# A two-layer attention kernel on one core: weight products behind their own loads, band values in pairs, first loads and statistics moved ahead of three stage borders

## The reference, cut to what matters

```python
x = L0_attn_x                                   # (2, 2048, 256)
xn = _layernorm(x, axis=-1)
s = _L0_attn_ref(xn, ...)                       # 16 heads of 16, full softmax over 2048 tokens
g = _silu(_L0_ffn_ref(xn, ...))                 # 8 experts, low rank, cumulative sum over tokens, forward + inverse branch
x = x + s * g
xn = _layernorm(x, axis=-1)
s = _L1_attn_ref(xn, ...)                       # the same heads, |q - k| <= 64
g = _silu(_L1_ffn_ref(xn, ...))                 # gated LoRA with 8 experts
x = x + s * g
```

## Time and profile before

| | us |
|---|---|
| median of 3 runs | 2538.43 (2525.03 to 2546.25) |
| the profiled execution, device time | 2525.01 |
| its span in the profile | 2523.4 |
| mean granted TensorE clock | 0.942 of full |
| PE busy | 2223.5 (88%) |
| DVE busy | 1840.8 (73%) |
| ACT busy | 1448.0 (57%) |
| POOL busy | 462.9 (18%) |

### The profile page before, as it was taken

One profiled execution on the slowest core, in us unless ns is written; L12 is line 12 of the kernel. 1 busy time (PEld: TensorE's weight loads), 2 busy tenths in 40 slices (PEclk: granted clock), 3 DMA queues, 4 the chain that ended last, 5 costly groups with the idle time before them and its releaser, 6 DMA issues. The chain is left out here.

```text
span 2523.4 us, 44312 instructions
## 1 busy us (share of the span) xinstructions
PE 2223.5 (88%) x14912; PEld 1229.1 (49%) x14912; DVE 1840.8 (73%) x3240; ACT 1448.0 (57%) x2165; POOL 462.9 (18%) x673
## 2 busy tenths in 40 slices
PE   4588689999999999999999999988999966799988
PEld 3456333333333333333333333327888855555578
DVE  1655589999999999999999999913443465798736
ACT  2344257777777777777777777771222222266643
POOL 0000000000000000000000000003554510266645
PEclk9799679999999999999999999998999988698889
DMA  3567820040230400500404102006666269876365
GB/s 121 198 237 260 137 26 3 12 55 3 34 33 5 62 5 8 60 3 21 47 5 51 16 5 62 3 5 189 159 164 180 67 239 333 150 148 139 82 183 161
DMA packets 189122, 231.81 MB, mean 92 GB/s; under 512 B 72721, under 2 KB 122769, under 8 KB 186065
## 3 DMA queue, kind: packets, MB, share of 16 engines
q1 hardware_dynamic: 176048, 210.46, 34.2%
q10 hardware_dynamic: 7184, 14.10, 3.0%
q0 software_dynamic: 5728, 5.00, 0.9%
HBM read 138.97 MB, written 89.13 MB: 90 GB/s over the span
## 5 line engine op out<-in xcount | busy, mean ns | idle before, releaser
L967 DVE TENSOR_REDUCE a_maxes<-a_ps_a 128x2 f32<-128x1024 f32 x1024 | 1202.2, 1221 | 112.8 <-PE a_ps_a L1088 109.0
L1032 ACT ACTIVATE a_prob<-a_ps_s 128x512 f32<-128x512 f32 (+1 forms) x1376 | 1036.2, 805 | 348.4 <-PE a_ps_s L1114 342.4
L1114 PE MATMUL a_ps_s<-a_Q,a_K 50*128 50x512 f32 x2048 | 593.4, 453 | 89.8 <-ACT a_prob L1032 89.7
L1088 PE MATMUL a_ps_a<-a_K,a_Q 48*128 48x512 f32 x2048 | 551.2, 455 | 25.2 <-DMA a_Q<-s_halves 14.1
L1126 PE MATMUL a_ps_o<-a_prob,a_V 128*17 128x512 f32 x4096 | 541.5, 601 | 0.1
L1114 PEld LDWEIGHTS a_ps_s<-a_Q,a_K 50*128 50x128 f32 x2048 | 277.2, 185 | 504.9 <-ACT a_prob L1032 456.9
L1088 PEld LDWEIGHTS a_ps_a<-a_K,a_Q 48*128 48x128 f32 x2048 | 245.1, 189 | 230.7 <-issue 107.9
L925 POOL DMA_DIRECT2D a_Q<-a_m_parts x128 | 64.3, 502 | 1282.3 <-DVE a_m_parts L959 1278.6
L1532 ACT ACTIVATE a_prob<-a_ps_s 128x512 f32<-128x512 f32 (+1 forms) x256 | 136.2, 583 | 128.0 <-PE a_ps_s L1623 124.6
L1473 DVE CUSTOM_DVE_ANT_0 a_scratch<-a_ps_a,k_mask 128x256 f32<-128x256 f32 (+1 forms) x512 | 176.7, 410 | 41.6 <-PE a_ps_a L1587 41.6
L1587 PE MATMUL a_ps_a<-a_K,a_Q 48*128 48x256 f32 (+1 forms) x512 | 124.1, 369 | 32.5 <-DMA a_Q<-s_halves 31.6
(11 more groups left out here) (184 smaller groups left out, 2212.2 us busy)
## 6 DMA issues: line engine op xcount, KB each, us to landing
s_halves<-p_parts SPq DMA_DIRECT2D x64, 512.0 KB, 5.2
s_xT<-p_xT SPq DMA_DIRECT2D x64, 256.0 KB, 4.4
a_K<-s_halves SPq DMA_DIRECT2D x63, 256.0 KB, 7.0
c_xT<-s_xT SPq DMA_DIRECT2D x48, 256.0 KB, 5.3
a_Q<-s_halves SPq DMA_DIRECT2D x186, 64.0 KB, 10.3
s_v<-p_v_out SPq DMA_DIRECT2D x16, 544.0 KB, 4.5
s_cT<-p_cT SPq DMA_DIRECT2D x32, 256.0 KB, 3.6
k_wb<-s_w SPq DMA_DIRECT2D x16, 512.0 KB, 7.7
```

Source lines behind the costliest of these rows:

```text
L967: nc.vector.tensor_reduce(maxes[:, :, slot, qt, kc], ps_a[:, o:o + 2 * CH].rearrange("p (z k) -> p z k", z=2), AX.X, ALU.max).then_inc(a_d ...
L1032: nc.scalar.activation(prob[:, ring:ring + len(t), :].rearrange("p r q -> p (r q)"), ps_s[:, bank:bank + len(t) * CH], ACT.Exp, scale=scal ...
L1088: last = nc.tensor.matmul(ps_a[:, o + side * CH:o + (side + 1) * CH], Q[rows, q0:q0 + P], K[rows, k0:k0 + CH], start=True, stop=True)
L1114: last = nc.tensor.matmul(ps_s[:, bank + x * CH:bank + (x + 1) * CH], K[rows, k0:k0 + P], Q[rows, q0:q0 + CH], start=True, stop=True)
```

## The change

Six edits:

- In `phase_weights` the loads are sorted into eleven groups with a semaphore each, the three arrays of the inverse first. PE waits for a group only before the product that needs it; the router products come before the expert products. The seven plain splits are done behind products 4, 8, 11 and 13. The bias rows have their own semaphore.
- The buffers and semaphores of a projection's first rows move out of `phase_project` into `row_buffers` (the rows lie in the weight buffer `wb`, which is idle then). The first two chunks of x are loaded, measured and rooted, and the first is normalised, inside `phase_weights`.
- The same is done for layer 1 in the last chunk of `phase_combine_experts`.
- The first 24 loads of K and Q for the band are issued near the end of `phase_project(layer 1)`, 12 (`first_halves`) and 12 (`second_halves`), half by SP and half by ACT.
- In the band, values are multiplied for two steps at a time, at even steps; ACT's copies go with them, PE's turns and DVE's normalisation follow at odd steps. RING, the number of buffers for exponentials, goes from 5 to 6.
- In the last two groups of the band SP loads the first four chunks of transposed tokens and two chunks of rows for `phase_combine_lora`.

```diff
+        loads = {
+            "inverse": [(square["WinvT"][:], "W_invT"), (square["WQ"][:], "W_Q"), (square["WK"][:], "W_K")],
+            "router": [(square["W1T"][:], "router_w1T")],
+            "Vf": [(wide["Vf"][:], "V_fwd")], "Vi": [(wide["Vi"][:], "W_inv_exp")],
+            "qkv0": [(raw_qkv[:, 0], "w_qkvT_0")],
...
+        PLAIN_AT = {4: (0,), 8: (1,), 11: (2,), 13: (3, 4, 5, 6)}
...
+            for g, group in loads.items():
+                for dst, key in group:
+                    sp.dma_start(dst, I[key].rearrange("(k p) n -> p k n", p=P)).then_inc(loaded[g], DMA)
+                if g in ("router", "Vi"):
+                    load_rows(sp, L, I["x"], 0, 0 if g == "router" else 1)
...
-            pe.wait_ge(loaded, DMA * n_loads)
+            have("inverse")
...
+            row_statistics(nc, dve, L, 0, 0, passed)
             for j in range(N_SPLIT):
...
+                for i in PLAIN_AT.get(j, ()):
+                    plain_low_part(i)
+                if j == 1:
+                    row_statistics(nc, dve, L, 0, 1, passed)
+                if j == 2:
+                    normalise_rows(nc, dve, L, 0, 0)
...
+        def first_halves(eng, side):
+            if KQ:
+                for m in range(4):
+                    wait_apart(eng, parts_stored[m], DMA * 2 * (NCH - 1), passed)
+                load_first(eng, S, KQ, side)
...
+                    if not more and u == 0:
+                        first_halves(sp, 0)
                     store_parts(sp, i, u)
                     if after:
                         store_turned(sp, *after)
+                    if not more and u == 1:
+                        second_halves(sp, 0)
                     store_values(sp, i, u)
...
+                    if not more:
+                        (second_halves if u else first_halves)(act, 1)
...
-    RING = 5
+    RING = 6
...
             def prefetch(g, k):
+                wait_apart(sp, s_ready, 2 * (KT * g + 2 * k + 2), passed)
                 if g + 2 < NG:
-                    wait_apart(sp, s_ready, 2 * (KT * g + 2 * k + 2), passed)
-                    load_next(sp, 0, g + 2, k)
+                    load_next(sp, S, KQ, 0, g + 2, k)
+                elif k < 4:
+                    for x in range(2):
+                        load_lora_turned(sp, S, KQ, (g + 2 - NG) * 2 + k // 2, k % 2, x)
+                elif g + 2 == NG:
+                    load_lora_rows(sp, KQ, KQ["x"], x_dram, k - 4)
...
-                if 0 <= s - LAG < STEPS:
-                    add_values(s - LAG)
-                if 0 <= s - LAG - 1 < STEPS:
-                    for cc in ends_at(s - LAG - 1):
-                        turn_output(cc)
+                if s % 2 == 0 and LAG < s < STEPS + LAG:
+                    for earlier in (s - LAG - 1, s - LAG):
+                        add_values(earlier)
+                if s % 2 == 1 and LAG + 1 < s:
+                    for earlier in (s - LAG - 2, s - LAG - 1):
+                        for cc in ends_at(earlier):
+                            turn_output(cc)
...
+                else:
+                    wait_apart(sp, mul1, FT * c + HALF_FT, passed)
+                    for u in range(2):
+                        load_rows(sp, L, out_dram, 0, u)
...
+                if c == CHUNKS - 1:
+                    for u in range(2):
+                        row_statistics(nc, dve, L, 0, u, passed)
                 for t in range(TT):
                     n = TT * c + t
+                    if c == CHUNKS - 1 and t == 1:
+                        normalise_rows(nc, dve, L, 0, 0)
```

More of the change, by code:

```diff
@@ L181, in _, with have @@
             last.then_inc(high, 1)
[L183 to L185 removed]
         @block.tensor
         def _(pe):
[L189 removed]
+            def have(g):
+                pe.wait_ge(loaded[g], DMA * len(loads[g]))
+            have("inverse")
             for m, src in ((0, WQ), (1, WK)):
@@ L197, in _ @@
             pe.wait_ge(high, 2)
+            have("router")
             j = 0
+            for t in range(DK):
+                for r, left in enumerate((WQ, WIQ)):
+                    for k in range(DK):
+                        o = (2 + j % 6) * CH + r * D
+                        last = nc.tensor.matmul(bank[:, o:o + D], left[:, k, t * P:(t + 1) * P],
+                                                square["W1T"][:, k, :], start=(k == 0),
+                                                stop=(k == DK - 1), skip_group_check=True)
+                last.then_inc(product, 1)
+                j += 1
             for left, right in ((WQ, "Vf"), (WIQ, "Vi"), (WK, "Wf"), (WIK, "Wi")):
+                have(right)
                 for t in range(DK):
@@ L208, in _ @@
                     j += 1
-            for t in range(DK):
-                pe.wait_ge(low, j - 5)
-                for r, left in enumerate((WQ, WIQ)):
-                    for k in range(DK):
-                        o = (2 + j % 6) * CH + r * D
-                        last = nc.tensor.matmul(bank[:, o:o + D], left[:, k, t * P:(t + 1) * P],
-                                                square["W1T"][:, k, :], start=(k == 0),
-                                                stop=(k == DK - 1), skip_group_check=True)
-                last.then_inc(product, 1)
-                j += 1
+            have("out")
             for half in range(4):
@@ new lines, in row_statistics @@
+def row_statistics(nc, dve, L, i, u, passed):
+    c = 2 * i + u
+    dve.wait_ge(L["x_loaded"][u], DMA * (i + 1))
+    for t in range(TT):
+        nc.vector.bn_stats(L["stats"][:, u, t], L["xn"][:, u, t]).then_inc(L["stat"], 1)
+    wait_apart(dve, L["stat"], (TT + 1) * c + TT, passed)
+    for t in range(TT):
+        last = nc.vector.bn_aggr(L["mean_var"][:, u, t], L["stats"][:, u, t])
+    last.then_inc(L["stat"], 1)
+    dve.wait_ge(L["stat"], (TT + 1) * (c + 1))
+    nc.vector.tensor_scalar(L["var_eps"][:, u], L["mean_var"][:, u, :, 1], EPS, None, ALU.add
+                            ).then_inc(L["eps_ready"], 1)
@@ L334, in phase_project @@
         ps_l = n.ps("ps_l", CH) if first else None
[L339 to L343 removed]
+        xn_ready = L["xn_ready"]
         t_ready = n.sem("t_ready")
@@ new lines, in load_first, with load_second, load_next @@
+def load_first(eng, S, KQ, side):
+    for k in range(PAIR + 1):
+        load_keys(eng, S, KQ, side, 0, 0, EARLY_K, k, KQ["early"])
+    for k in range(PAIR + 1):
+        load_queries(eng, S, KQ, side, 0, 0, k, KQ["early"])
+def load_second(eng, S, KQ, side):
+    for k in range(PAIR + 1):
+        load_keys(eng, S, KQ, side, 0, EARLY_K, T, k, KQ["loaded"][0])
+    for k in range(PAIR + 1):
+        load_queries(eng, S, KQ, side, 0, 1, k, KQ["loaded"][0])
+def load_next(eng, S, KQ, side, g, k):
+    done = KQ["loaded"][g % BAND_BUFS]
+    if k % 2 == 0:
+        load_keys(eng, S, KQ, side, g, 0, T, k // 2, done)
+    else:
+        load_queries(eng, S, KQ, side, g, 0, k // 2, done)
+        load_queries(eng, S, KQ, side, g, 1, k // 2, done)
@@ L2011, in _ @@
                         bias(c, ft // 2 - 1)
+                if c == CHUNKS - 1:
+                    for u in range(2):
+                        inverse_root(pool, W, L, u, u)
                 for t in range(TT):
```

370 lines of the change are left out of this document (178 added, 192 removed).

## The result

| | before | after |
|---|---|---|
| median, us | 2538.4 (2525.0 to 2546.3, 4 runs) | 2471.4 (2462.9 to 2482.3, 4 runs) |
| ratio, with its 95% interval | | 0.976 (0.972 to 0.980) |
| profiled execution: device time, span | 2525.0, 2523.4 | 2464.9, 2463.2 |
| mean granted TensorE clock in it | 0.942 | 0.952 |

The change makes the kernel faster, and by more than was forecast: 2471 lies 7 us under the low end of the range, 2478. Run again twice, the changed kernel stood at 0.9759 and 0.9763 of the kernel before, so some 60 us are the change's own; the 67 us of the first medians are those and a little luck. By the sum's own measure, span against span, 37 us were forecast and 60.2 came.

What follows compares the result with a forecast made beforehand. Loads bound the first 27.4 us; in the band DVE is the limit at 2.4 GHz, PE at 1.2. Sum: −33.2 − 9.2 + 0.8 + 11 − 6.4 = −37.0, from 2525.0 to 2488 us; range 2478 to 2522.

Steps and rivals of the forecast that it cites:

- Weights and first projection: Start of kernel: PE starts after three arrays, fewer splits remain, rows are already normalised; −33.2 us (−27 to −36).
- rival 3: Weights stage: PE runs the weight products at 1.2 GHz, stopping between load groups; −23 us, 2515; chance 0.05.
- Experts to second projection: Border after the experts: statistics and normalisation fit DVE's idle time, PE starts with the stage; −9.2 us (−4 to −9.5).
- The band's first loads: Projection's end and band's start: moved loads cost 15.8 us, gain 15; net +0.8 us (−9 to +6).
- rival 2: Band's start: moved loads cost 15.8 us and win nothing, group 1 still waits; −22 us, 2516; chance 0.14.
- The price in the tail: Late second projection: 24 moved loads, 3.1 MB, lengthen the stage's end by 15.8 us, the upper end taken.
- Values in pairs: Band: −4.5 for fewer trips, +9.6 for later copies at borders, +6 for the clock; +11 us in all (−20 to +25).
- the 6 us for more falls of the clock: Band: longer waits pull the clock to 1.2 GHz at two borders more, 3 us each; +6 us.
- The −4.5 in this term: Band at 1.2 GHz: pairs take away one trip in four, 0.15 us a step over some 30 steps.
- LoRA stage: Start of LoRA stage: tokens already there, attention rows arrive before PE turns them; −6.4 us (−4 to −6.8).
- rival 1: Band loses nothing: later copies still land in time, clock stays up; band −12, total −60, 2478 us; chance 0.17.
- rival 4: Band: clock falls at the first border and doesn't come back; slower than before, +23 us, 2561; chance 0.05.

## Why the prediction was wrong, step by step

- **Weights and first projection**, −33.2: −35.8 to PE's first transpose. PE started at 7.00, where 9 was taken from a range of 6.5 to 11: the three arrays were in before most else. That is 2 of the 2.6 us that are missing. No product waited for a group of loads, and PE ran at 0.98 of the clock from 7 to 42.5: rival 3 is out. That the start is worth its full length the run with one wait for all weights shows (25 us).
- **Experts to second projection**, −9.2: −10.0. Right.
- **The band's first loads**, +0.8: +1.4 at the tail with the head in it, −3.9 behind, together −2.5; and the run that undoes the move finds no difference. The forecast that they pay for themselves holds, and rival 2, by which they cost 15.8 us and win nothing, is out. The price in the tail was a few us too high: the band's head became 10.5 us shorter and the stretch as a whole 1.4 longer, so the tail cost 12 us, not 15.8.
- **Values in pairs**, +11: this is the step that failed. It measured −8 (0.9967 alone, −2 to −15). The prediction said that the copies of the maxima would be issued a step later, 1.6 us, and that there was no slack, so that each of six borders would wait that much longer (+9.6). The first half holds: they begin 1.5 us later. At the border of the earlier trace rows there was no slack either: PE goes on as the last copy lands. What fails is that a later beginning was taken for a later landing. In the kernel before, the copies stand 0.94 us behind a load of keys, and the last lands 9.2 us behind their beginning; a step later they stand 2.6 us behind that load and need 7.9. So the landing moves by 0.2 us (12.3 to 12.5 behind the turn) and not by 1.6. PE's waits for a_m_parts in the whole band are 6.9 us before, 7.0 with pairs alone, and 4.9, 3.0 and 5.0 in the three profiles of the changed kernel.
- With it fell the 6 us for more falls of the clock: the low stretches sum to 65 us before, 41 with pairs alone, and 34, 20 and 37 in three profiles of the changed kernel. Where the 8 us come from is open: the waits for copies are no shorter with pairs alone, only the low stretches are.
- The −4.5 in this term, 0.15 us a step for fewer trips of PE at the low clock, rests on no row; no run shows it, and single values four steps behind do as well as pairs.
- A price of pairs at the borders is there once the load is out of the way: pairs then cost 16 us against single values. But it is not the one predicted. The copies land as early; the two loads that SP issues behind them are late (7.3 us of waits against 0.6), and the low stretches sum to 34 us against 10.
- **LoRA stage**, −6.4: PE starts 0.4 us behind the stage's begin in place of 6.4, and the rest takes 1.3 us more, −4.8 in all. The tail was costed at nothing. PE waits for no attention rows in either profile; 1.1 of the 1.3 us lie behind its last product (6.7 us before, 7.8 after), and no run says why.
- **The rivals**: rival 1, that the band loses nothing, is near to what happened, and its 2478 is where the ratio puts the kernel. That the numbers meet is in part luck: the copies are still waited for and the clock still falls, the band won less than the 12 us of the rival, and most of the smaller terms won more than forecast. The range ended exactly at that value, so that the scatter of the runs by itself was enough to leave it. Had the rival been let in with the scatter that the three runs before showed, some 10 us to either side, the low end would have been near 2468. In rival 4 the clock falls at the first border of the band and stays down; no profile shows that.

Not settled: what pairs, or a fourth step of lag, win by. Both give slack and both move the copies away from the load ahead of them. It shows as shorter low stretches in the profiles with pairs and not in the one with four steps, and no run separates these causes. Nor does a run move ACT's load of keys, which stands 1 us ahead of the copies in the kernel before, as SP's does.

## What to carry to other kernels

Cost a moved transfer by when it lands, and look at the rows around it in its queue: what stood just ahead of it may be the price, and a move away from that can pay for being late. What stands behind it moves too, and may be waited for next. Before a change of the order of compute, try moving the one load that shares the queue with a critical small copy; here one number in a wait was worth 28 us, more than the pairs. And where short waits are followed by a low clock, as here at four borders of six, a wait's price can be several times its length: look at the clock of the stretch behind it. Not every short wait has one.

## What was not expected of the hardware

- What four small copies cost depends on their neighbours. In the last group, with no load in the 10 us ahead, they took 2.4 to 2.7 us to issue and the last landed 4.0 to 4.2 us behind their beginning (kernel before, and pairs alone on it). With SP's load of keys 0.9 us ahead it was 4.0 and 9.2, with it 2.6 ahead 3.2 and 7.9, with it 4.8 ahead 3.6 and 6.5 (medians). The distance to that load is not all: with it some 3 us ahead, on the kernel before, it was 3.4 and 8.1, and there ACT's own load of keys still stood 0.8 us ahead. The Trainium skill ("DMA: Bandwidth & Descriptors", section "Two DMAs through the same engine are not ordered") has it that within one queue of one DMA engine descriptors start in order; that small copies wait their turn behind a large load fits it, the size of the price comes from the rows alone.
- The scatter between runs of one kernel, 2519 to 2554 us for the one before, goes with the granted clock: over its 54 runs 0.01 of clock is 18 us.
- In the kernel before with the fifth load sooner, 5 us less of waits for copies came with 22 us less of time in the band, most of it the stretches at 1.2 GHz that no longer followed a border. The 0.84 us waits for a_neg_max, of which there are more (6.9 us against 4.8), were followed by none but one of 3 us.
